# A state-space scan on TensorE, its steps paired across head groups, with the second step's output product moved to the end of the same slot

## What is computed

```python
H, P, HID, N, G, K, CS = (32, 64, 256, 128, 1, 4, 64)
gate, hBC, dt = ...                      # x @ W_in.T + b_in, split
hBC = silu(conv(hBC))                    # 4 taps along the rows
h, Bm, Cm = ...                          # split of hBC
A_cum = jnp.cumsum(A_c, axis=-1)         # A * dt, in chunks
Y_diag = einsum(Cm Bm * exp(segsum(A_c)), h * dt)      # inside a chunk
states = states * decay + einsum(Bm * decay, h * dt)   # from chunk to chunk
Y_off = einsum(Cm, states) * exp(A_cum)
y = (Y_diag + Y_off) + D * h
g = y * silu(gate)
g = g * rsqrt(mean(g * g, axis=-1) + EPS) * norm_w
return g @ W_out.T + b_out
```

## Time and profile before

| | |
|---|---|
| runs | 2261.38, 2265.36, 2267.99 us; median 2265.36 |
| profiled execution | 2262.73 us, of which 2261.0 is the span of the core's instructions |
| granted clock, mean | 0.986 |
| TensorE busy | 2124.2 us (94%), 13681 matmuls |
| VectorE, ScalarE, GpSimd busy | 1575.2 (70%), 1266.4 (56%), 1414.6 (63%) |
| the mixer's stage | about 150 to 1380 us of the span |
| TensorE in 600 to 800 us | 194.92 us busy, clock 1.00 |
| VectorE, ScalarE, GpSimd in 600 to 800 us | 169.56, 150.09, 154.80 us busy |

### The profile page before, as it was taken

The page is one execution under the profiler, slowest core; times in us unless marked ns, Lnnn a source line. Parts: engine busy times, 40 slices in busy tenths (PEclk is TensorE's granted clock), DMA queues, the critical chain, the costliest instruction groups (busy, mean ns, idle before and its releaser), DMA issues. The chain is left out here.

```text
span 2261.0 us, 43811 instructions
## 1 busy us (share of the span) xinstructions
PE 2124.2 (94%) x13681; PEld 1685.8 (75%) x13681; DVE 1575.2 (70%) x3408; ACT 1266.4 (56%) x2754; POOL 1414.6 (63%) x1248
## 2 busy tenths in 40 slices
PE   4878999999999999999999998999989989999997
PEld 2446777777777777777777776877744779999997
DVE  5778888888888888888888884676766853333332
ACT  2456777777777777777777772222235653333332
POOL 1325777777777777777777775777764624444443
PEclk9999999999999999999999999999999999999999
DMA  9854445545554455454545544886473065232221
GB/s 321 333 135 119 135 144 147 152 137 146 145 156 135 144 148 151 139 146 143 150 140 145 141 133 140 254 268 217 151 261 118 1 222 137 48 50 47 46 46 24
DMA packets 193458, 328.83 MB, mean 145 GB/s; under 512 B 49043, under 2 KB 135188, under 8 KB 192980
## 3 DMA queue, kind: packets, MB, share of 16 engines
q1 hardware_dynamic: 135972, 227.40, 34.1%
q0 software_dynamic: 26640, 53.38, 9.1%
q10 hardware_dynamic: 30624, 45.25, 6.5%
HBM read 240.19 MB, written 86.53 MB: 145 GB/s over the span
## 5 line engine op out<-in xcount | busy, mean ns | idle before, releaser
L1014 DVE SCALAR_TENSOR_TENSOR m_cv<-m_hp,conv,m_cv 128x256 f32<-128x256 f32 x864 | 416.7, 482 | 112.2 <-ACT m_cv L913 91.0
L840 POOL TENSOR_TENSOR m_er<-m_er,m_cT 128x1024 f32<-128x1024 f32 x128 | 302.3, 2362 | 43.7 <-DVE m_ar L1021 43.7
L951 ACT ACTIVATE m_ar<-m_ar,m_ta 128x128 f32<-128x128 f32 x1024 | 318.9, 391 | 0.8
L1102 PE MATMUL m_hp<-xnT,wpj 128*128 128x259 f32 x1152 | 304.7, 387 | 7.8 <-PEq L145 4.5
L1110 PE MATMUL m_gp<-xnT,wpj 128*128 128x256 f32 x1024 | 268.2, 384 | 11.2 <-ACT m_gT L931 11.2
L1538 PE MATMUL e_u<-e_xgT,xnT 128*128 128x128 f32 x2272 | 266.9, 276 | 1.0 <-ACT xnT L1476 1.0
L1102 PEld LDWEIGHTS m_hp<-xnT,wpj 128*128 128x128 f32 x1152 | 214.1, 192 | 68.7 <-issue 28.3
L1538 PEld LDWEIGHTS e_u<-e_xgT,xnT 128*128 128x128 f32 x2272 | 260.9, 193 | 1.3 <-ACT xnT L1476 1.2
L847 POOL TENSOR_TENSOR m_hdd<-m_hdt,m_tb 128x512 f32<-128x512 f32 x128 | 131.0, 1043 | 193.6 <-DVE m_hdt L1029 193.6
L931 ACT ACTIVATE m_gT<-m_gp,bias 128x256 f32<-128x256 f32 x256 | 121.4, 474 | 230.6 <-PE m_gp L1110 178.5
L1161 PE MATMUL m_out<-wo,m_gT 128*128 128x256 f32 x1024 | 242.9, 380 | 0.0
(11 more groups left out here) (338 smaller groups left out, 4260.8 us busy)
## 6 DMA issues: line engine op xcount, KB each, us to landing
m_ar<-acum_rows_dram SPq DMA_DIRECT2D x512, 128.0 KB
m_er<-eacum_rows_dram SPq DMA_DIRECT2D x128, 512.0 KB, 4.3
rows_by_slot<-blank_rows ACTq DMA_DIRECT2D x1, 18576.0 KB, 81.0
e_xg<-rows_by_slot ACTq DMA_DIRECT2D x131, 129.0 KB
m_xrow<-xn_rows SPq DMA_DIRECT2D x32, 512.0 KB, 5.1
arena<-y_rows SPq DMA_DIRECT2D x16, 1024.0 KB, 7.2
arena<-in_w SPq DMA_DIRECT2D x5, 1024.0 KB
wpj<-in_w_proj SPq DMA_DIRECT2D x1, 4352.0 KB, 23.6
```

The source lines that it names most:

```text
L840: g.tensor_tensor(er[:, t], er[:, t], middle(cT[:, t * P:(t + 1) * P], HQ), ALU.mult).then_inc(scaled.sem, 1)
L951: ins = a(row, row, ACT.Exp, bias=ta[:, t, q * HQ + h:q * HQ + h + 1])
L1014: v_.scalar_tensor_tensor(o, hp[n % 2][:, j:j + BLK], conv[:, c, j:j + 1], o, ALU.mult, ALU.add).then_inc(tapped.sem, 1)
L1102: ins = mm(hp[n % 2][:, 0:PW], w_proj[:, kd, col:col + P], xpad[:, kd, ds(i * BLK, PW)], start=kd == 0, stop=kd == KD - 1)
```

## The change

Slot n now does two steps of different head groups: `older(n - 1)`, the second half block of the group before (called a), and `newer(n - 1)`, the first half block of group `u` (called b). The tables of the block (`ta`, `tb`, `gm`, `btok`) get a third slot for t = 1, since a step of the block before may still need them. On TensorE the products of both steps come first, then the update of a, the second late convolution product, the output product of a, the update of b, and last the output product of b. On VectorE a's `finish` comes ahead of its `grow`, and the copy of the C rows behind those of `tb`, `gm` and `btok`. On GpSimd one `scale` comes at the end of the slot, for the next. `add_up` moves from a block's first slot to its second, `DEPTH` from 2 to 3. The waits in `from_state` and `age` on the state's growth for t = 0 reach back to the block before.

```diff
-DEPTH = 2
+DEPTH = 3
...
+def older(m):
+
+    return divmod(m - 1, NQ) + (1,) if 0 < m <= NB * NQ else None
+
+
+def newer(m):
+
+    return divmod(m, NQ) + (0,) if 0 <= m < NB * NQ else None
+
+
+def pair(m):
+
+    return [s for s in (older(m), newer(m)) if s]
+
+
+def kept(i, t):
+
+    return 1 + i % 2 if t else 0
...
# SyncE
-                    for t in range(TB):
-                        s = q * TB + t
-                        off.wait(sp, i, s - 1)
...
+                    for i, q, t in pair(n):
+                        decay_rows(i, q, t)
+                        row_matrix(i * STEPS + q * TB + t + TB)
...
# GpSimd
+                    a, b, last = older(n - 1), newer(n - 1), newer(n - 2)
+                    if b:
+                        mixed.wait(pool, b[0], b[1] * TB + 1)
+                        scale(*b)
+                    if last:
+                        add_squares(*last)
+                    if a:
+                        weigh(*a)
+                    if b:
+                        weigh(*b)
+                    if a:
+                        age(*a)
+                    if b:
+                        age(*b)
+                    if last and last[1] == NQ - 1:
+                        fold_squares(last[0], 0)
                     if u:
-                        mixed.wait(pool, i, q * TB + TB)
-                        scale(i, q, 0)
-                        weigh(i, q, 0)
-                        weigh(i, q, 1)
-                        age(i, q, 0)
-                        scale(i, q, 1)
...
+                        scale(*u, 1)
+                    if a:
+                        add_squares(*a)
+                        if last_of(a):
+                            fold_squares(a[0], 1)
...
# ScalarE
-                        if c == 1 and v:
-                            square(*v, 1)
...
+                        if c == 1 and last:
+                            square(*last)
+                    for step, chunk in ((older(n), 0), (newer(n), 1)):
+                        lead = chunk + 1
+                        if step:
+                            exps(*step, range(0, lead))
+                        if late[chunk] is not None:
+                            first_tap(w[0], late[chunk])
+                        if step:
+                            exps(*step, range(lead, HQ))
+                    step = older(n - 1)
...
-                    if u:
-                        square(*u, 0)
...
+                    if step:
+                        square(*step)
+                    if last_of(older(n - 2)):
+                        i = older(n - 2)[0]
                         ss_done.wait(act, i, 1)
...
# VectorE
-                    if u:
-                        grow(*u, 0)
-                        finish(*u, 0)
+                    if a:
+                        finish(*a)
+                        grow(*a)
                     if w:
                         taps(w[0], late[1])
-                    if u:
-                        finish(*u, 1)
-                        grow(*u, 1)
+                    if b:
+                        finish(*b)
+                        grow(*b)
...
# TensorE
                     if w:
                         project(w[0], late[0])
-                    if u:
-                        from_state(*u, 0)
-                        inside(*u, 0)
-                        update(*u, 0)
+                    for step in pair(n - 1):
+                        from_state(*step)
+                        inside(*step)
+                    if a:
+                        update(*a)
                     if w:
                         project(w[0], late[1])
-                    if v:
-                        project_out(*v, 1)
-                    if u:
-                        from_state(*u, 1)
-                        inside(*u, 1)
-                        update(*u, 1)
-                    if v and v[1] == NQ - 1:
-                        add_up(v[0])
-                    if u:
-                        project_out(*u, 0)
+                    if a:
+                        project_out(*a)
+                    if b:
+                        update(*b)
+                    if b:
+                        project_out(*b)
+                    if last_of(older(n - 2)):
+                        add_up(older(n - 2)[0])
```

More of the change, by code:

```diff
@@ L707, in at, with both, last_of @@
             return (i, q) if 0 <= i < NB else None
-        body(at(0), at(1), at(2))
+        body(n, at(0), at(1))
+def older(m):
[6 more added lines that the diff above has]
+    return 1 + i % 2 if t else 0
+def both(i):
+    return slice(0, 2 + i % 2, 1 + i % 2)
+def last_of(step):
+    return step is not None and step[1] == NQ - 1 and step[2] == TB - 1
 def ssd_phase(nc, sem, k, xpad, w_proj, w_out, bias, conv, d_col, dt, tabs, acum_dram, eacum_dram, ss, mo_dram,
@@ L950, in exps, with body @@
                         row = ar[:, s % 4, h, :]
-                        ins = a(row, row, ACT.Exp, bias=ta[:, t, q * HQ + h:q * HQ + h + 1])
+                        ins = a(row, row, ACT.Exp, bias=ta[:, kept(i, t), q * HQ + h:q * HQ + h + 1])
                     if heads[-1] == HQ - 1:
                         ins.then_inc(exped.sem, 1)
-                def body(w, u, v):
-                    soon, late = fresh(w[1]) if w else ([None] * 4, [])
+                def body(n, w, u):
+                    soon, late = fresh(w[1]) if w else ([None] * 4, [None] * 2)
+                    last = newer(n - 2)
                     if u:
@@ L967, in body @@
                             first_tap(w[0], soon[c])
-                        if c == 1 and v:
-                            square(*v, 1)
[L970 to L974, removed]
-                    if v and v[1] == NQ - 1:
-                        i = v[0]
+                        if c == 1 and last:
[9 more added lines that the diff above has]
+                    step = older(n - 1)
+                    if last_of(step):
+                        i = step[0]
                         outd.wait(act, i, STEPS)
@@ L1053, in finish, with body @@
                     v_.tensor_tensor(gg, gg, y1[:].rearrange("p (c l) -> p c l", l=P), ALU.mult).then_inc(gated.sem, 1)
-                def body(w, u, v):
-                    soon, late = fresh(w[1]) if w else ([None] * 4, [])
+                def body(n, w, u):
+                    soon, late = fresh(w[1]) if w else ([None] * 4, [None] * 2)
+                    a, b = older(n - 1), newer(n - 1)
                     if w and w[1] == 0:
-                        exped.wait(dve, w[0], 0)
-                        v_.tensor_copy(ta[:], tabs[:, ds(w[0] * TB, TB), 0, :]).then_inc(ta_done.sem, 1)
+                        i = w[0]
+                        exped.wait(dve, i, -1)
+                        v_.tensor_copy(ta[:, both(i)], tabs[:, ds(i * TB, TB), 0, :]).then_inc(ta_done.sem, 1)
                     if u and u[1] == 0:
@@ L1127, in from_state @@
                     scaled.wait(pe, i, s + 1)
-                    grown.wait(pe, i, s)
+                    grown.wait(pe, i, s if t else s + TB - STEPS)
                     y3d.wait(pe, i, s - 1)
```

82 lines of the change are left out of this document (37 added, 45 removed).

## The result

The changed kernel takes 2411.73 us (median; 2409.89 to 2414.63), the kernel before 2264.07: ratio 1.0652, interval 1.0631 to 1.0672, slower by 148 us. The forecast was 2391, the range 2352 to 2436. The profiled execution took 2409.89 us against 2262.73, with a mean granted clock of 0.978 against 0.986.

What follows compares the result with a forecast made beforehand. The prediction took TensorE's own work to bound the kernel. Its terms, 85 + 25 + 13 + 4 - 1, gave +126 us on the profiled 2262.73, so 2389, and 2391 us for the median; range 2352 to 2436.

Steps and rivals of the forecast that it cites:

- TensorE's stream is the path: TensorE is busiest, 17.80 us a slot; a wait put into its stream is paid in full unless it replaces another.
- The new wait: Before output b, TensorE awaits VectorE's gating: 1.41 us idle, +1.37 us a slot, 62 slots, 85 us.
- The saved switch: On TensorE, one change between 64-column and full-width weights per slot falls away, saving 0.14 us.
- the rule by which the saving would be nothing: Skill's rule: TensorE weight loads overlap products only when row groups differ; no switch special, sum 9 us higher.
- VectorE against GpSimd: GpSimd's adding of squares starts 0.32 us before VectorE's gating of b, delaying it 0.80 us in 31 slots: 25 us.
- the rival in which VectorE gets in first: VectorE's gating of b starts before GpSimd's adding, so the 25 us go: 2366 us; chance 0.24.
- The small terms: Sum of squares' new place 16 x 0.8 = 13 us, C rows' copy 15 x 0.28 = 4, extra drain slot -1.
- 2366 - 13: Range's lower end, given as 2352: no GpSimd blocking of the gating and the sum-of-squares term nothing.
- The clock: Rival: TensorE's clock falls after the 2.21 us gaps, 1.7 us each in 31 slots, 53 us, 2444; chance 0.14.
- A drop in the middle of the stage: Sign of being wrong: the clock drops mid-stage, where the forecast expected granted clock 1.00.
- run 126: Not a run's number: 126 us is the forecast's summed slowdown over the whole profiled execution, 2262.73 to 2389.
- TensorE doesn't wait: Rival: b's gated product is there by 15.94 us of the slot, so pairs save 9 us: 2256; chance 0.06.

Runs made afterwards that it cites:

- e8_no_early: e6_defer_add and e5_ss_early together, plus VectorE's mix of a ahead of its copies at a block's start; 2254.96 us, 0.9959 of the kernel before.
- e3_add_later: Changed kernel with GpSimd adding the squares of a one slot later, behind its first scaling; 2371.22 us.
- e1_defer: Changed kernel with the output product of b taken one slot later, and ScalarE's copy of a block's result moved with it; 2310.09 us.
- e2_gate_first: Changed kernel with VectorE's gating of b ahead of the slot's last taps, growth of b's state behind them; 2306.25 us.
- e6_defer_add: e1_defer with the edit of e3_add_later added; 2281.53 us.
- e5_ss_early: Changed kernel with the sum of squares product right behind the second convolution product instead of last in the block's second slot; 2398.64 us.
- e4_fill: Changed kernel with six needless 128-column products on TensorE between update and output of b; 2390.43 us.

## Why the prediction was right, and where it was off

- **TensorE's stream is the path.** Right: the gaps of 116.3 us came with 148 us of time, and each run that shortened a gap shortened the kernel.
- **The new wait.** Right in place and size: 1.39 against 1.41 idle. In the slot of 633.31 the second convolution product starts 13.19 after the slot's start instead of 12.38, since the slot's front was late; from the end of its record to the slot's end it is 6.64 us, where the forecast had 5.75 + 0.80 = 6.55. In the slot of 613.84, whose front is as before, the second output product ends 19.11 us after the start (632.95), where the forecast had 19.17.
- **The saved switch.** Right in sign, too small in size: 0.35 a slot in the rows of e8_no_early, not 0.14; the rule by which the saving would be nothing is out here. The first inner and the second state products take 0.87 and 0.88 there, where the forecast had 0.93 each, and the update of b takes 0.86 behind an output product, where it had 0.96. In the changed kernel half of the difference of 0.21 counts: the second convolution product starts 12.27 us after the slot's start (626.11 in the slot of 613.84) instead of 12.38. The other half, the shorter update, only lengthens the wait behind it.
- **VectorE against GpSimd.** Right, and the rival in which VectorE gets in first is out: GpSimd led by 0.27 us (forecast 0.32), and e3_add_later gave 22 of the 25 us back. The Trainium skill (SBUF — State Buffer, Who interferes with whom) has the two engines share a pair of ports that the first one holds for its whole instruction; the trace agrees in this kernel, e1_defer and e2_gate_first, each with the blocked gating ending 0.54 to 0.55 after GpSimd's operation.
- **The small terms.** Behind the sum of squares the second convolution product starts 13.19 us after the slot's start instead of 12.27: 0.92 late, where the forecast had 0.8. ScalarE's table load and silu stand right behind it (633.49 to 635.60 in its rows), as argued. The copy of the C rows was not run apart from the other edits; in a block's first slot the transposes' first wait for VectorE's scaled chunks is 0.49 us (row of 680.59) against 0.28 before (632.41), 0.21 more where the forecast had 0.28. The lower end of the range, 2366 - 13, is 2353 and not 2352.
- **The clock.** Here the sum fell short. I held the fall for a rival of all or nothing and took the granted clock as 1.00 in the forecast. In fact it fell eleven times in the stage, roughly 1.7 us each. A drop in the middle of the stage was named as a sign of being wrong, and that sign came. The time still lies in the range, since the range left room for falls in most of the blocked slots; fewer than half had one. Over one block the rows add up: the four slots from 569.48 to 654.18 take 84.70, the block of 572.74 to 647.77 before took 75.03; 9.67 more, of which the forecast's terms explain 4 x 1.37 + 2 x 0.80 + 0.80 + 0.28 = 8.16 and the one fall in it 1.7, together 0.2 too much. Over the run 126 + 18.7 = 145 of the 147.2 between the profiled executions. The step that failed is thus the term for the clock, put at 0 and measured at 18.7.
- **TensorE doesn't wait.** Out: it waits in every slot.
- **What my experiments' expectations lacked.** For e1_defer and e2_gate_first I took the output product's wait for the whole cost of the late gating. VectorE's next work, behind the same gating, was not in the sum; it cost 29 us (e1_defer against e6_defer_add).

## What to carry to other kernels

To run a step's last product in the slot in which its operand is made, compare the clock faces of producer and consumer first: three links behind a late product made 1.4 us that nothing covered, once a slot. When a wait is taken away, look at what stands behind the producer on its own engine, for that is late next; here the deferred product alone won back 102 of the 148 us, and the moved additions on GpSimd 29 more. And price each new gap on TensorE twice, by its length and by the clock that may fall behind it.

## What the runs showed that was not expected

Gaps of the same length did not have the same effect on the clock. In the changed kernel it fell behind the 2.29 us gap at 589.11 (0.66 over the next five us) but not behind the 2.23 us gap at 652.35, whose products take 1.99. Over the stage all eleven falls stand behind one of the 29 gaps of over 2 us, and none behind the 34 shorter ones. In e3_add_later the two falls come with two of the five gaps of over 2 us that are left. In e5_ss_early, where only the sum of squares moved, 18 falls come on 28 such gaps. What tells the gaps with a fall from those without is left open; filling them with products down to 0.90 us (e4_fill) ended all falls of the stage.
